# A six-layer attention pipeline on one core: the step's order rewritten on TensorE, ScalarE and VectorE

## The chip, the cores and the metric

The kernel runs on one core of a Trainium2 chip. The metric is the device time of one execution in microseconds (us). A core has five engines with a queue of instructions each: TensorE (PE; its weight loads are shown apart, as PEld), VectorE (DVE), ScalarE (ACT), GpSimd (POOL) and SyncE (SP), which here only starts DMAs. Each works its queue in order; they meet at semaphores. PE writes its results to PSUM, eight banks of 128 x 512 float32.

## The reference, cut to what matters

The program computes a chain of cross attentions and feed-forward networks on x (32 sequences of 128 tokens, 128 features). The change is in one part of it, six layers of local attention, each with a gated feed-forward network:

```
for i in range(6):
    x = attn_layer(shift_tokens(x), Wqkv[i], q_scale[i], k_scale[i], Wo[i]) + x
    x = ffn_layer(shift_tokens(x), ln_g[i], ln_b[i], W1[i], b1[i], W2[i], b2[i]) + x

def attn_layer(x, Wqkv, qs, ksc, Wo):        # 16 heads of 64
    q, k, v = jnp.split(x @ Wqkv, 3, -1)
    q = l2norm(q) * qs;  k = l2norm(k) * ksc
    q = q * cos * scale + rotate_half(q) * sin * scale
    k = k * cos / scale + rotate_half(k) * sin / scale
    return local_attention(q, k, v) @ Wo      # softmax, window of 32

def ffn_layer(x, g, bln, W1, b1, W2, b2):    # 128 -> 2 x 341 -> 128
    xn = (x - mu) / jnp.sqrt(var + 1e-05) * g + bln
    a, gate = jnp.split(xn @ W1 + b1, 2, -1)
    return a * gelu(gate) @ W2 + b2
```

shift_tokens moves the upper 64 features down by one token.

## The kernel before, in words

`layer_stack` holds the six layers. A tile is one sequence (128 tokens), so a layer has 32 tiles and the stack 192; four tiles are a quad, the unit of the feed-forward network. All engines run the same software pipeline (`layered_loop`): in step m each engine does pieces of work for several tiles, tile m (projection and rotation), m-1 (norms, turning of q and k), m-2 (values, scores, exponentials), m-3 and m-4 (turned probabilities, weighted values, output), m-5 and m-6 (token shift, layer norm). The order of the pieces in a step is written by hand for each engine in its `step` function; there is no scheduler. Every fourth step (k % 4 == 3) is a quad step, which also does the feed-forward network of an earlier quad. Of each layer the first 8 steps are unrolled (16 in the first), the others run in a hardware loop of 8 steps. After tile 191 there are 8 closing steps without new tiles.

The pieces that matter here, with their lines:

- PE. `project(m, j)` (L2646) makes the q or k unit j of tile m, 128 x 512 (units 0 and 1 are q, 2 and 3 are k). `project_values(m-2, half)` (L2663) makes half of the values. Both write to PSUM banks 0 and 1, which each result must leave before the next one. `shift(m-5)` (L2801) is a small matmul for the shifted tokens. `scores` (L2719, L2725), `turn_qk` (L2693), `turn_probs` (L2756), `weighted_values` (L2776), `output` (L2791), `turn_x` (L2614); in quad steps `turn_quad` (L2811), `hidden` (L2827, L2828), `ffn_output` (L2835).
- ACT. `squares` (L2334) reads a projected unit; `evacuate_values` half 1 (L2312), `evacuate_qk` (L2300), `evacuate_probs` (L2306), `evacuate_heads` half 0 (L2318), `exponentials` (L2326, four per group), `log_norms` and `over_norms` (L2340, L2345), `high_half` (L2363), which takes the result of `shift`, and `evacuate_x` (L2369, L2370), which writes the transposed input xsT of tile m.
- DVE. `maxima` (L2448), `evacuate_values` half 0 (L2496), `cosines` (L2462) and `sines` (L2473) of each unit, which wait for that unit's `squares`; `sums_of_squares` (L2480), `one_over_sums` (L2455), `statistics` (L2517), which waits for `high_half`, and `aggregate` (L2522).
- POOL. Its step, which the change leaves alone, runs one step of index ahead: `to_unit(n-3, 1)` (L2261), `keep(n-6)` (L2248), `to_unit(n-3, 3)`, `copy_for_values(n-3)` (L2235, xvT from xsT), `normalise(n-4, 0)` (L2268), `rotate(n-2, 2)` (L2254), `normalise(n-4, 1)`, `low_half` (L2241), `rotate(n-2, 3)`, `to_unit(n-2, 2)`, `to_unit(n-2, 0)`, `fetch(n)` (L2229), `rotate(n-1, 0)`, `rotate(n-1, 1)`, `normalise(n-4, 3)`, `normalise(n-4, 2)`.

xsT has two buffers, so `evacuate_x` of tile m+1 may write only when `copy_for_values` of tile m-1 has read the same buffer:

```
def evacuate_x(b, w, live):
    if live(b):
        act.wait_ge(turned, b + 1)
        wait(act, xvT_ready, b - 1)
```

`turn_qk` and `turn_probs` share banks 2 and 3, so `turn_qk(m-2, half 1)` waits until ACT has moved out what `turn_probs(m-4, half 1)` wrote just before it:

```
waits_alone(pe, env, (unit_ready[half], b + 1), (unit_ready[2 + half], b + 1),
            (probT_ready[1][0], b - 1), (probT_ready[1][1], b - 1))
```

## Time and profile before

| | |
|---|---|
| median of 3 runs | 4495.72 us (4494.81 to 4501.11) |
| the profiled execution | 4496.44 us, span 4494.6 us |
| busy over the span | PE 4166.5 us (93%), DVE 3761.2 (84%), ACT 3599.0 (80%), POOL 3142.6 (70%) |
| the six layers' projections (L2646) | from 563 us to 3764 us of the span |
| one regular step in the loop | 14.38 us, one quad step 23.00 us (2041.34 to 2055.72 and 2055.72 to 2078.72 us of the span) |

A busy share over the whole span mixes the six layers with the other parts. The six layers are one pipeline with a fixed period, so the trace is best read there one step at a time, from one `turn_x` on PE to the next.

### The profile page before, as it was taken

The page shows a single profiled execution, that of the slowest core. Times are in us where ns is not written, and L with a number is a line of the kernel's source. Part 1 is how long each engine was busy: PE and PEld are TensorE (multiplying, and loading weights), DVE is VectorE, ACT ScalarE, POOL GpSimd, SP SyncE. Part 2 cuts the span into 40 slices and gives each one's busy share as a digit, 9 for nine tenths or more (in the row PEclk, how much of TensorE's full clock was granted, in tenths as well). Part 3 has the DMA queues.
Part 4 walks back from the last instruction along what each step waited for, and adds up shares of the span by engine and source line. Part 5 has one row for each costly group of instructions (what it writes and reads, how often), then busy time and mean ns, then how long its engine had stood idle before and what let it go on. Part 6 is the DMA issues. An engine that isn't in the chain of part 4 may idle for free. (4 is left out here: it accounts for less than half of the span.)

```text
span 4494.6 us, 151390 instructions
## 1 busy us (share of the span) xinstructions
PE 4166.5 (93%) x51005; PEld 2759.3 (61%) x51005; DVE 3761.2 (84%) x9029; ACT 3599.0 (80%) x12939; POOL 3142.6 (70%) x4201
## 2 busy tenths in 40 slices
PE   6949999999999999999999999999999999677885
PEld 3426656666666666666666666666666666455543
DVE  4779989889889889889888889888889886688497
ACT  6938878888888888888888888888888887688335
POOL 2422288888879788889888788888888876444162
PEclk9969999999999999999999999999999999888886
DMA  2000000000000000000000000000000000000000
GB/s 63 0 21 1 0 8 2 2 3 16 13 3 2 3 21 8 3 3 9 14 8 3 3 12 12 8 3 3 16 12 3 3 3 2 1 0 0 29 1 19
DMA packets 38699, 37.87 MB, mean 8 GB/s; under 512 B 11382, under 2 KB 30068, under 8 KB 37748
## 3 DMA queue, kind: packets, MB, share of 16 engines
q1 hardware_dynamic: 38004, 28.97, 2.3%
q8 instruction: 391, 6.41, 0.6%
q14 instruction: 304, 2.49, 0.2%
HBM read 26.86 MB, written 2.10 MB: 6 GB/s over the span
## 5 line engine op out<-in xcount | busy, mean ns | idle before, releaser
L2326 ACT ACTIVATE stack_prob<-ps,stack_shift_by 128x128 f32<-128x128 f32 x3072 | 1078.7, 377 | 5.5 <-DVE stack_shift_by L2448 4.7
L2254 POOL TENSOR_TENSOR stack_qk<-stack_qk,stack_rsin 128x512 f32<-128x512 f32 x768 | 968.6, 1272 | 40.9 <-DVE stack_rsin L2473 40.9
L2261 POOL TENSOR_TENSOR stack_qk<-stack_qk,stack_inv 128x512 f32<-128x512 f32 x768 | 793.4, 1044 | 255.8 <-ACT stack_inv L2345 255.8
L2646 PE MATMUL ps<-local_wqkv,stack_xsT 128*128 128x512 f32 x1536 | 797.5, 601 | 7.1 <-DVE stack_vals L2496 3.0
L2268 POOL TENSOR_TENSOR stack_prob<-stack_prob,stack_rs 128x512 f32<-128x512 f32 x768 | 791.1, 1041 | 1.8 <-DVE stack_rs L2455 1.8
L2326 ACT ACTIVATION_READ_ACCUMULATOR stack_prob<-ps,stack_shift_by 128x1 f32 x3072 | 668.9, 218 | 0.0
L2448 DVE TENSOR_REDUCE stack_shift_by<-ps 128x4 f32<-128x512 f32 x768 | 524.3, 683 | 109.3 <-PE ps L2725 105.2
L2473 DVE TENSOR_TENSOR stack_rsin<-ps,stack_sin_t 128x256 f32<-128x256 f32 x1536 | 571.7, 413 | 0.0
L2462 DVE TENSOR_TENSOR stack_qk<-ps,stack_cos_t 128x512 f32<-128x512 f32 x768 | 525.2, 684 | 41.1 <-ACT stack_sq L2334 40.7
L2480 DVE TENSOR_REDUCE stack_ss<-stack_sq 128x8 f32<-128x512 f32 x768 | 514.0, 670 | 0.7 <-ACT stack_sq L2334 0.7
L2334 ACT ACTIVATE stack_sq<-ps 128x512 f32<-128x512 f32 x768 | 467.7, 609 | 50.8 <-PE ps L2646 43.9
L2306 ACT ACTIVATE stack_probT<-ps 128x512 f32<-128x512 f32 x768 | 427.4, 630 | 31.5 <-PE ps L2756 31.5
L2663 PE MATMUL ps<-local_wqkv,stack_xvT 128*128 128x512 f32 x768 | 433.4, 646 | 1.9 <-issue 1.6
L2776 PE MATMUL ps<-stack_probT,stack_vals 128*64 128x128 f32 x6144 | 425.6, 281 | 9.1 <-issue 7.0
L2776 PEld LDWEIGHTS ps<-stack_probT,stack_vals 128*64 128x64 f32 x6144 | 331.6, 138 | 165.7 <-issue 152.9
L2300 ACT ACTIVATE stack_qkT<-ps 128x512 f32<-128x512 f32 x384 | 230.9, 601 | 234.7 <-PE ps L2693 234.5
L2791 PE MATMUL ps<-local_wo,stack_oT 128*128 128x128 f32 x3072 | 389.0, 280 | 0.2 <-issue 0.2
L2791 PEld LDWEIGHTS ps<-local_wo,stack_oT 128*128 128x128 f32 x3072 | 361.2, 192 | 34.3 <-issue 24.5
L2646 PEld LDWEIGHTS ps<-local_wqkv,stack_xsT 128*128 128x128 f32 x1536 | 257.6, 191 | 179.0 <-issue 97.6
L2725 PE MATMUL ps<-stack_qkT 64*64 64x64 f32 (+1 forms) x12288 | 343.2, 232 | 0.0
L2725 PEld LDWEIGHTS ps<-stack_qkT 64*64 64x64 f32 x12288 | 311.1, 135 | 0.0
L2756 PEld LDWEIGHTS ps<-ident,stack_prob 64*128 64x128 f32 x6144 | 223.0, 139 | 94.8 <-issue 91.7
(342 smaller groups left out, 8601.7 us busy)
## 6 DMA issues: line engine op xcount, KB each, us to landing
local_wqkv<-L_ffn_Wqkv SPq DMA_DIRECT2D x30, 256.0 KB, 2.7
local_wo<-L_ffn_Wo SPq DMA_DIRECT2D x6, 512.0 KB, 4.5
out<-quantised_res SPq DMA_DIRECT2D x8, 256.0 KB, 2.3
local_w<-L_ffn_W SPq DMA_DIRECT2D x6, 341.0 KB
local_wqkv<-L_ffn_Wqkv SPq DMA_DIRECT2D x1, 1536.0 KB, 6.4
early_L_decay<-c_decay SPq DMA_DIRECT2D x1, 1024.0 KB, 10.7
local_w<-L_ffn_W SPq DMA_DIRECT2D x12, 64.0 KB
load_raw<-L_ffn_w SPq DMA_DIRECT2D x8, 64.0 KB, 2.0
```

What stands on the lines that cost most here:

```text
L2254: nc.gpsimd.tensor_tensor(qk[w][:, j, :, :], qk[w][:, j, :, :], rsin[j % 2][:, :, :], ALU.add).then_inc(rot_ready, 1)
L2261: nc.gpsimd.tensor_tensor(qk[w][:, j, :, :], qk[w][:, j, :, :], bcast(inv[:, w, 8 * j:8 * j + 8].unsqueeze(2), [P, 8, LH]), ALU.mult).then ...
L2268: nc.gpsimd.tensor_tensor(prob[w][:, g, :, :], prob[w][:, g, :, :], bcast(rs[:, w, HG * g:HG * g + HG].unsqueeze(2), [P, HG, P]), ALU.mult ...
L2326: last = nc.scalar.activation(prob[w][:, g, j, :], ps[:, 4 + g % 2, j * P:(j + 1) * P], ACT.Exp, bias=shift_by[:, w, h:h + 1], accum_out=s ...
L2448: nc.vector.tensor_reduce(shift_by[:, w, HG * g:HG * g + HG], bank, AX, ALU.max, negate=True).then_inc(shift_by_ready, 1)
L2462: nc.vector.tensor_tensor(qk[w][:, j, :, :], bank, bcast(cos_t[:, j // 2, :].unsqueeze(1), [P, 8, LH]), ALU.mult)
L2473: last = nc.vector.tensor_tensor(rsin[j % 2][:, :, o], bank[:, :, x], bcast(sin_t[:, j // 2, o].unsqueeze(1), [P, 8, 32]), ALU.mult)
L2480: nc.vector.tensor_reduce(ss[:, w, 8 * j:8 * j + 8, 0], sq[j % 2][:, :, :], AX, ALU.add).then_inc(ss_summed, 1)
L2646: nc.tensor.matmul(proj_bank(j), xsT[w][:, :], wqkv[:, 512 * j:512 * j + 512], start=True, stop=True).then_inc(proj_ready, 1)
L2725: last = nc.tensor.matmul(ps[part, 4 + p, j * P + keys.start:j * P + keys.stop], qkT[w][r, half, 0, j, part], qkT[w][r, half, 1, j, keys], ...
L2776: last = nc.tensor.matmul(PV[LH * p:LH * p + LH, j * P:(j + 1) * P], vals[w][:, LH * h:LH * h + LH], probT[w][:, 2 * half + p, j, :], star ...
L2791: last = nc.tensor.matmul(OUT[:, 0:P], oT[w][:, c, :], wo[:, c, :], start=c == 0, stop=c == 7)
```

## The change

The work of a step is the same, and no instruction on data is added or taken away; it is put in another order on PE, ACT and DVE. POOL and the DMAs keep theirs. On PE both value projections of tile m-2 and units 0 and 1 of tile m now stand together, behind the weighted values; unit 2 stands late, before the output. The units' banks change from (1, 0, 0, 1) to (0, 1, 0, 1), so that half 0 of the values and unit 0 use bank 0 one behind the other, and half 1 and unit 1 bank 1. The feed-forward network's hidden parts 0 and 2 use banks 0 and 6, part 1 banks 2 and 3. The waits follow the new order.

```diff
@@ -2161,14 +2161,14 @@
     PV, OUT = ps[:, 6, :], ps[:, 7, :]
 
 
-    UNIT_BANK = (1, 0, 0, 1)
+    UNIT_BANK = (0, 1, 0, 1)
     HALF_KEYS = (slice(0, LH), slice(32, P))
 
     def proj_bank(j):
         return ps[:, UNIT_BANK[j], :]
 
     def hidden_banks(c):
-        return (ps[:, 2, :], ps[:, 3, :]) if c != 1 else (ps[:, 1, :], ps[:, 6, :])
+        return (ps[:, 2, :], ps[:, 3, :]) if c == 1 else (ps[:, 0, :], ps[:, 6, :])
 
     def live_quad(q):
         return not isinstance(q, int) or 0 <= q < NQUADS
@@ -2387,36 +2387,38 @@
             def step(m, q, k, live, layer):
                 u, v = k % 2, 1 - k % 2
                 quad = k % QUAD == QUAD - 1 and live_quad(q - 2)
+                evacuate_x(m, u, live)
+                evacuate_probs(m - 4, u, 1, 0, live)
+                evacuate_probs(m - 4, u, 1, 1, live)
                 evacuate_heads(m - 4, u, 0, live)
-                evacuate_x(m, u, live)
+                exponentials(m - 2, u, 0, live)
+                exponentials(m - 2, u, 1, live)
+                evacuate_values(m - 2, u, 1, live)
+                log_norms(m - 1, v, live)
                 evacuate_qk(m - 2, u, 1, 0, live)
-                exponentials(m - 2, u, 0, live)
                 squares(m, u, 0, live)
-                log_norms(m - 1, v, live)
-                high_half(m - 5, v, live)
                 over_norms(m - 1, v, live)
                 squares(m, u, 1, live)
-                exponentials(m - 2, u, 1, live)
+                high_half(m - 5, v, live)
+                if quad:
+                    quad_input(q - 2, layer)
                 evacuate_probs(m - 3, v, 0, 1, live)
                 evacuate_probs(m - 3, v, 0, 0, live)
-                evacuate_values(m - 2, u, 1, live)
+                log_variance(m - 6, u, live)
                 if quad:
-                    quad_input(q - 2, layer)
-                log_variance(m - 6, u, live)
-                squares(m, u, 2, live)
-                over_deviation(m - 6, u, live)
-                if quad:
+                    over_deviation(m - 6, u, live)
                     gates(q - 2)
                     exponentials(m - 2, u, 2, live)
                     exponentials(m - 2, u, 3, live)
                     evacuate_qk(m - 1, v, 0, 0, live)
+                    squares(m, u, 2, live)
                 else:
+                    exponentials(m - 2, u, 2, live)
+                    over_deviation(m - 6, u, live)
+                    squares(m, u, 2, live)
+                    exponentials(m - 2, u, 3, live)
                     evacuate_qk(m - 1, v, 0, 0, live)
-                    exponentials(m - 2, u, 2, live)
-                    exponentials(m - 2, u, 3, live)
                 squares(m, u, 3, live)
-                evacuate_probs(m - 3, v, 1, 0, live)
-                evacuate_probs(m - 3, v, 1, 1, live)
             layered_loop(act, NB, step)
 
         @block.vector
@@ -2547,44 +2549,42 @@
                 if isinstance(m, int) and m % NB == 0 and live(m):
                     tables(m // NB)
                 maxima(m - 2, u, 0, live)
+                maxima(m - 2, u, 1, live)
+                bound_norms(m - 1, v, live)
                 evacuate_qk(m - 2, u, 1, 1, live)
+                evacuate_heads(m - 4, u, 1, live)
                 evacuate_values(m - 2, u, 0, live)
-                bound_norms(m - 1, v, live)
-                maxima(m - 2, u, 1, live)
                 one_over_sums(m - 3, v, 2, live)
                 one_over_sums(m - 3, v, 3, live)
+                one_over_sums(m - 2, u, 0, live)
+                statistics(m - 5, v, live)
+                one_over_sums(m - 2, u, 1, live)
+                aggregate(m - 5, v, live)
                 cosines(m, u, 0, live)
                 sines(m, u, 0, live)
+                maxima(m - 2, u, 2, live)
+                maxima(m - 2, u, 3, live)
                 cosines(m, u, 1, live)
                 sines(m, u, 1, live)
-                statistics(m - 5, v, live)
-                sums_of_squares(m, u, 0, live)
-                one_over_sums(m - 2, u, 0, live)
-                sums_of_squares(m, u, 1, live)
-                aggregate(m - 5, v, live)
-                evacuate_heads(m - 4, u, 1, live)
-                maxima(m - 2, u, 2, live)
-                one_over_sums(m - 2, u, 1, live)
                 if quad:
-                    maxima(m - 2, u, 3, live)
-                    sums_of_squares(m, u, 2, live)
                     gated(q - 2, 0, layer)
-                    cosines(m, u, 2, live)
+                    sums_of_squares(m, u, 0, live)
                     gated(q - 2, 1, layer)
-                    sines(m, u, 2, live)
+                    sums_of_squares(m, u, 1, live)
                     gated(q - 2, 2, layer)
                     residual(m - 4, u, layer, live)
                     norm(m - 6, u, (k - 6) % RING, live)
                     evacuate_qk(m - 1, v, 0, 1, live)
                     quad_residual(q - 2, layer)
                 else:
+                    sums_of_squares(m, u, 0, live)
                     evacuate_qk(m - 1, v, 0, 1, live)
-                    maxima(m - 2, u, 3, live)
-                    sums_of_squares(m, u, 2, live)
+                    sums_of_squares(m, u, 1, live)
                     residual(m - 4, u, layer, live)
                     norm(m - 6, u, (k - 6) % RING, live)
-                    cosines(m, u, 2, live)
-                    sines(m, u, 2, live)
+                cosines(m, u, 2, live)
+                sines(m, u, 2, live)
+                sums_of_squares(m, u, 2, live)
                 cosines(m, u, 3, live)
                 sines(m, u, 3, live)
                 sums_of_squares(m, u, 3, live)
@@ -2623,25 +2623,17 @@
                         keep_busy(nc, env, SPARE, FILL[(b, j)])
                     if j == 0:
                         pe.wait_ge(xsT_ready, b + 1)
-                        wait(pe, rot_step, 4 * b)
-                        if isinstance(b, int):
-                            wait(pe, vals_ready[1], b - 2)
-                            wait(pe, rot_step, 4 * b - 3)
-                    elif j == 1:
                         wait(pe, vals_ready[0], b - 1)
                         if isinstance(b, int):
                             wait(pe, rot_step, 4 * b - 1)
-                            wait(pe, rot_step, 4 * b - 2)
-                    elif j == 2:
-                        wait(pe, rot_step, 4 * b + 2)
-                        if isinstance(b, int):
-                            wait(pe, vals_ready[0], b - 1)
-                            wait(pe, rot_step, 4 * b - 1)
-                    else:
+                    elif j == 1:
                         wait(pe, vals_ready[1], b - 1)
                         if isinstance(b, int):
-                            wait(pe, rot_step, 4 * b + 1)
                             wait(pe, rot_step, 4 * b)
+                    elif j == 2:
+                        wait(pe, rot_step, 4 * b + 1)
+                    else:
+                        wait(pe, rot_step, 4 * b + 2)
                     new_layer(b, wq_loaded[j])
                     nc.tensor.matmul(proj_bank(j), xsT[w][:, :], wqkv[:, 512 * j:512 * j + 512],
                                      start=True, stop=True).then_inc(proj_ready, 1)
@@ -2649,16 +2641,9 @@
...
-                    if half == 0:
-                        wait(pe, rot_step, upto(4 * b + 7, 4 * TOTAL))
-                        if isinstance(b, int):
-                            wait(pe, rot_step, upto(4 * b + 6, 4 * TOTAL))
-                            wait(pe, vals_ready[0], b)
-                    else:
-                        wait(pe, rot_step, upto(4 * b + 9, 4 * TOTAL))
-                        if isinstance(b, int):
-                            wait(pe, rot_step, upto(4 * b + 8, 4 * TOTAL))
-                            wait(pe, vals_ready[1], b)
+                    wait(pe, rot_step, upto(4 * b + 7 + half, 4 * TOTAL))
+                    if isinstance(b, int):
+                        wait(pe, vals_ready[half], b)
...
@@ -2815,12 +2800,14 @@
...
+                        pe.wait_ge(rot_step, upto(4 * m + 1, 4 * TOTAL))
+                        if isinstance(q, int):
+                            pe.wait_ge(vals_ready[0], upto(m - 1, TOTAL))
+                        pe.wait_ge(oT_ready[1], upto(m - 3, TOTAL))
+                        pe.wait_ge(xT_ready, q + 1)
+                    elif c == 1:
-                        pe.wait_ge(xT_ready, q + 1)
-                    elif c == 1:
-                        pe.wait_ge(vals_ready[1], upto(m - 1, TOTAL))
-                        pe.wait_ge(oT_ready[1], upto(m - 3, TOTAL))
...
@@ -2847,25 +2834,26 @@
                 weighted_values(m - 4, u, 0, live)
                 scores(m - 2, u, 0, live)
                 turn_qk(m - 2, u, 1, live)
+                weighted_values(m - 4, u, 1, live)
                 project_values(m - 2, u, 0, live)
+                project_values(m - 2, u, 1, live)
                 project(m, u, 0, live)
                 shift(m - 5, v, live)
                 project(m, u, 1, live)
-                weighted_values(m - 4, u, 1, live)
-                turn_probs(m - 3, v, 0, live)
-                project_values(m - 2, u, 1, live)
                 if quad:
                     turn_quad(q - 2, m, k // QUAD)
-                project(m, u, 2, live)
+                turn_probs(m - 3, v, 0, live)
                 scores(m - 2, u, 1, live)
                 if quad:
                     hidden(q - 2, m, layer)
                     output(m - 4, u, live)
-                    wait_alone(pe, env, h_ready, 3 * (q - 2) + 3)
+                    wait_alone(pe, env, h_ready, 3 * (q - 2) + 2)
                     turn_qk(m - 1, v, 0, live)
                     ffn_output(q - 2)
+                    project(m, u, 2, live)
                 else:
                     turn_qk(m - 1, v, 0, live)
+                    project(m, u, 2, live)
                     output(m - 4, u, live)
                 project(m, u, 3, live)
             layered_loop(pe, NB, step)
```

PE, a regular step in the unrolled part of a layer, from `turn_qk` of tile m-2 (qk0) to the scores: xvT0 feeds the value projections, xsT0 the q and k projections. Before:

```order
L2693 MATMUL ps<-ident,stack_qk0 128x64 x16
L2663 MATMUL ps<-local_wqkv,stack_xvT0 128x512
L2646 MATMUL ps<-local_wqkv,stack_xsT0 128x512
L2801 MATMUL ps<-stack_xnew,shift 128x64
L2646 MATMUL ps<-local_wqkv,stack_xsT0 128x512
L2776 MATMUL ps<-stack_probT0,stack_vals0 64x128 x8
L2756 MATMUL ps<-ident,stack_prob1 128x64 x16
L2663 MATMUL ps<-local_wqkv,stack_xvT0 128x512
L2646 MATMUL ps<-local_wqkv,stack_xsT0 128x512
L2719 MATMUL ps<-band2,identb 64x4x64 x2
```

The same place now (line numbers are those of the changed kernel):

```order
L2678 MATMUL ps<-ident,stack_qk0 128x64 x16
L2761 MATMUL ps<-stack_probT0,stack_vals0 64x128 x8
L47 REGISTER_ALU
L2648 MATMUL ps<-local_wqkv,stack_xvT0 128x512
L47 REGISTER_ALU
L2648 MATMUL ps<-local_wqkv,stack_xvT0 128x512
L2638 MATMUL ps<-local_wqkv,stack_xsT0 128x512
L2786 MATMUL ps<-stack_xnew,shift 128x64
L2638 MATMUL ps<-local_wqkv,stack_xsT0 128x512
L2741 MATMUL ps<-ident,stack_prob1 128x64 x16
```

The weighted values moved ahead of the projections and the second value projection ahead of both units; unit 2 left this place.

DVE, a regular step from the copy of the values (vals) to `sines` of unit 1, with the semaphores that each waits for. Before:

```order
L2496 COPY stack_vals1<-ps 128x512 [waits stack_vproj_ready]
L2485 TENSOR_REDUCE stack_bounded<-stack_ss 128x32 [waits stack_ss_summed]
L2448 TENSOR_REDUCE stack_shift_by<-ps 128x4 [waits stack_scores_ready]
L2455 RECIPROCAL stack_rs<-stack_sm 128x4 [waits stack_exp_ready] x2
L2462 TENSOR_TENSOR stack_qk1<-ps,stack_cos_t 128x512 [waits stack_qk_turned,stack_sq_ready]
L2473 TENSOR_TENSOR stack_rsin0<-ps,stack_sin_t 128x8x32 [waits stack_rot_ready,stack_sq_ready]
L2473 TENSOR_TENSOR stack_rsin0<-ps,stack_sin_t 128x8x32
L2462 TENSOR_TENSOR stack_qk1<-ps,stack_cos_t 128x512 [waits stack_qk_turned,stack_sq_ready]
L2473 TENSOR_TENSOR stack_rsin1<-ps,stack_sin_t 128x8x32 [waits stack_rot_ready,stack_sq_ready]
```

Now:

```order
L2498 COPY stack_vals1<-ps 128x512 [waits stack_vproj_ready]
L2457 RECIPROCAL stack_rs<-stack_sm 128x4 [waits stack_exp_ready] x3
L2519 BN_STATS stack_stats<-stack_xs 128x6 [waits stack_shift_ready,stack_half_ready]
L2457 RECIPROCAL stack_rs<-stack_sm 128x4 [waits stack_exp_ready]
L2524 BN_AGGR stack_moments<-stack_stats 128x2 [waits stack_stats_ready]
L2464 TENSOR_TENSOR stack_qk1<-ps,stack_cos_t 128x512 [waits stack_qk_turned,stack_sq_ready]
L2475 TENSOR_TENSOR stack_rsin0<-ps,stack_sin_t 128x8x32 [waits stack_rot_ready,stack_sq_ready]
L2475 TENSOR_TENSOR stack_rsin0<-ps,stack_sin_t 128x8x32
L2450 TENSOR_REDUCE stack_shift_by<-ps 128x4 [waits stack_scores_ready] x2
L2464 TENSOR_TENSOR stack_qk1<-ps,stack_cos_t 128x512 [waits stack_qk_turned,stack_sq_ready]
L2475 TENSOR_TENSOR stack_rsin1<-ps,stack_sin_t 128x8x32 [waits stack_rot_ready,stack_sq_ready]
```

Both maxima of groups 0 and 1 now stand ahead of the copy, `statistics` (BN_STATS) stands ahead of the first cosines where it stood behind the sines of unit 1, and the maxima of groups 2 and 3 stand between units 0 and 1.

ACT, from the last `squares` of a step to the exponentials of group 0 in the next; probT0 are the turned probabilities, xsT0 the transposed input. Before:

```order
L2334 ACTIVATE stack_sq1<-ps 128x512 [waits stack_ss_summed,stack_proj_ready]
L2306 ACTIVATE stack_probT0<-ps 128x8x64 [waits stack_prob_turned] x2
L2318 ACTIVATE stack_oT0<-ps 128x512 [waits stack_pv_ready]
L2367 REGISTER_ALU
L2369 ACTIVATE stack_xsT0<-ps 64x128 [waits stack_xvT_ready,stack_turned]
L2370 ACTIVATE stack_xsT0<-ps 64x127
L2299 REGISTER_ALU
L2300 ACTIVATE stack_qkT0<-ps 128x8x64 [waits stack_qk_turned]
L2326 ACTIVATE stack_prob0,stack_sm<-ps,stack_shift_by 128x128 [waits stack_shift_by_ready]
```

Now:

```order
L2334 ACTIVATE stack_sq1<-ps 128x512 [waits stack_ss_summed,stack_proj_ready]
L2367 REGISTER_ALU
L2369 ACTIVATE stack_xsT0<-ps 64x128 [waits stack_xvT_ready,stack_turned]
L2370 ACTIVATE stack_xsT0<-ps 64x127
L2306 ACTIVATE stack_probT0<-ps 128x8x64 [waits stack_prob_turned] x2
L2318 ACTIVATE stack_oT0<-ps 128x512 [waits stack_pv_ready]
L2326 ACTIVATE stack_prob0,stack_sm<-ps,stack_shift_by 128x128 [waits stack_shift_by_ready]
```

`evacuate_x`, with its wait for xvT, now stands ahead of the evacuation of the turned probabilities.

## Rows read from the trace of the kernel before

**Rows 1.** Windows: stretch, its us, busy us (instructions) by engine, PE's granted clock, DMA.

```profile
2041.34:2055.72 14.38, 14.38 (x201) 9.85 (x200) 13.83 (x34) 12.97 (x53) 14.03 (x17) 1.00 0.01 3
2055.72:2078.72 23.00, 23.00 (x241) 15.05 (x240) 17.85 (x41) 18.94 (x62) 17.58 (x22) 1.00 0.01 2
```

**Rows 2.** Timeline of PE, regular step: start, us, engine, line, tiles, count.

```profile
2044.16 0.71 PE L2693 MATMUL ps<-ident,stack_qk 64*128 64x64 f32 x16
2044.80 1.13 PE L2663 MATMUL ps<-local_wqkv,stack_xvT 128*128 128x512 f32 x2
2045.77 1.02 PE L2646 MATMUL ps<-local_wqkv,stack_xsT 128*128 128x512 f32 x2
2046.62 0.33 PE L2801 MATMUL ps<-stack_xnew,shift 128*128 128x64 f32 x2
2046.79 1.08 PE L2646 MATMUL ps<-local_wqkv,stack_xsT 128*128 128x512 f32 x2
2047.80 1.09 PE L2776 MATMUL ps<-stack_probT,stack_vals 128*64 128x128 f32 x16
```

**Rows 3.** Timeline of DVE, the same step.

```profile
2045.97 0.69 DVE L2496 COPY stack_vals<-ps 128x512 f32<-128x512 f32 x1 [0.16 <-PE ps L2663]
2046.70 0.68 DVE L2448 TENSOR_REDUCE stack_shift_by<-ps 128x4 f32<-128x512 f32 x1
2047.30 0.23 DVE L2455 RECIPROCAL stack_rs<-stack_sm 128x4 f32<-128x4 f32 x2
2047.53 0.69 DVE L2462 TENSOR_TENSOR stack_qk<-ps,stack_cos_t 128x512 f32<-128x512 f32 x1
2048.14 0.75 DVE L2473 TENSOR_TENSOR stack_rsin<-ps,stack_sin_t 128x256 f32<-128x256 f32 x2
2050.06 0.28 DVE L2517 BATCH_NORM_STATS2 stack_stats<-stack_xs 128x6 f32<-128x128 f32 x1
```

**Rows 4.** Timeline of ACT, the same step.

```profile
2042.41 1.14 ACT L2306 ACTIVATE stack_probT<-ps 128x512 f32<-128x512 f32 x2
2043.84 0.30 ACT L2369 ACTIVATE stack_xsT<-ps 64x128 f32<-64x128 f32 x1
2044.15 0.27 ACT L2370 ACTIVATE stack_xsT<-ps 64x127 f32<-64x127 f32 x1
2047.52 0.21 ACT L2363 ACTIVATE stack_xs<-ps 128x64 f32<-128x64 f32 x1
2047.91 0.60 ACT L2334 ACTIVATE stack_sq<-ps 128x512 f32<-128x512 f32 x1
```

**Rows 5.** Timeline of POOL, the same step and the next's start.

```profile
2048.05 2.04 POOL L2261 TENSOR_TENSOR stack_qk<-stack_qk,stack_inv 128x512 f32<-128x512 f32 x2 [0.35 <-ACT stack_inv L2345]
2050.29 2.50 POOL L2254 TENSOR_TENSOR stack_qk<-stack_qk,stack_rsin 128x512 f32<-128x512 f32 x2
2057.15 0.29 POOL L2235 COPY stack_xvT<-stack_xsT 128x128 f32<-128x128 f32 x1
```

**Rows 6.** Timeline of PE, a quad step.

```profile
2064.80 0.60 PE L2811 MATMUL ps<-ident,XN 128*128 128x128 f32 x4
2067.14 1.13 PE L2827 MATMUL ps<-XN,local_w 128*128 128x512 f32 x2
2077.86 1.02 PE L2646 MATMUL ps<-local_wqkv,stack_xsT 128*128 128x512 f32 x2
```

**Rows 7.** Timeline of PE, the two steps behind the loop's jump.

```profile
2011.09 0.32 PE L2614 MATMUL ps<-ident,stack_xin 128*128 128x128 f32 x1 [0.98 <-issue]
2026.78 0.30 PE L2614 MATMUL ps<-ident,stack_xin 128*128 128x128 f32 x1
```

**Rows 8.** Windows where PE waited: in the layers' start, in a later part.

```profile
592.00:596.00 4.00, 1.82 (x21) 0.95 (x19) 3.80 (x8) 3.30 (x18) 3.83 (x6) 1.00 0.00 0
3940.00:3944.00 4.00, 2.12 (x16) 1.71 (x20) 4.00 (x8) 3.97 (x8) 1.61 (x2) 0.93 0.00 0
3944.00:3948.00 4.00, 4.00 (x96) 3.53 (x90) 2.80 (x6) 3.29 (x7) 2.75 (x10) 0.65 0.00 0
```

## The prediction

> **What bounds the kernel now.** I read the windows of single steps first, then the timeline of each engine inside one of them. In a regular step of 14.38 us PE is busy for all 14.38, DVE for 13.83, POOL for 14.03, ACT for 12.97; in the quad step of 23.00 us only PE is full [rows 1]. So the order before is bound by PE in both kinds of step, and the other engines' waits are short: 0.16 us of DVE ahead of the copy of the values [rows 3], 0.35 us of POOL ahead of `to_unit` [rows 5]. Two things follow. A better order of PE's work can only win what PE loses between its pieces, not idle time, since there is none. And DVE and POOL have 0.55 and 0.35 us to spare in a regular step, so an order that makes either wait longer than that makes the step longer, unless PE's work hides it, which it cannot: it is a loop of waits that sets the period then, not a busy engine.
>
> **What PE gains.** A pair of 512-column passes that comes behind small tiles takes 0.97 us from its start to the next (2044.80 to 2045.77), one behind another pair of the same shape 0.85 (2045.77 to 2046.62); the one ahead of the weighted values takes 1.01 (2046.79 to 2047.80) [rows 2]. The new order has about one such border less per step (both value projections and units 0 and 1 form one run; unit 2 runs into the output). I take 0.10 us a step, from the 0.12 between 0.97 and 0.85. The Trainium skill, TensorEngine Tiling (Array Packing), Key Properties, says that changing the tiling mode drains TensorE; these rows agree, and by that rule alone the change would be a small gain, the faster rival below.
>
> **What the order costs: a chain inside the step.** I call E the end of DVE's copy of value half 0.
> - Unit 0 now uses bank 0 right behind that half, so P0 (unit 0 of tile m) cannot start before E. Before, bank 1 was free for it and it started 0.97 us behind V0 with no wait.
> - PE: P0 0.96 (behind a wait I let it pay the border), shift 0.17, P1 to its end 1.08: 2.21 us [rows 2].
> - ACT: `squares` of unit 1 0.49 until `high_half` starts, which now stands behind it, and 0.21 for that: 0.70 [rows 4].
> - DVE: `statistics` now stands ahead of all cosines and waits for `high_half`.
> With three handoffs of 0.04 us each DVE gets to `statistics` 3.03 us after E. Between the two it has only three reciprocals, 0.3 us at 0.23 for two [rows 3]. So it waits 2.7 us in every regular step. DVE alone then needs 13.83 + 2.7 = 16.5 us a step.
>
> **The chain goes on and closes.** From `statistics` DVE does: it 0.28 less overlap, a reciprocal and `aggregate`, together 0.38; cosines 0 0.61; sines 0 0.66; maxima 2 and 3 at 0.60; cosines 1 0.61; sines 1 0.75: 4.2 us [rows 3]. Before, the sines of unit 1 came early, and the two maxima after them. POOL's `rotate(m, 1)` waits for these sines, and behind it in POOL's unchanged order stand two `normalise`, `to_unit`, `keep`, `to_unit` and `copy_for_values(m-1)`. From the second rotation's start (2050.29 plus half of 2.50) to the end of that copy (2057.15 + 0.29) is 5.90 us, without a wait in it [rows 5]. ACT's `evacuate_x(m+1)` needs that copy, since it writes the buffer which the copy reads. Before, it stood behind the evacuation of the probabilities and the heads; now it is first in the step, and everything of ACT's step is queued behind it. So follow on ACT 0.58 for `evacuate_x` and 1.12 for the two evacuations of probabilities: 1.70 [rows 4]. PE's `turn_qk(m-1, half 1)` needs banks 2 and 3 from those: 0.64, then the weighted values 1.02 (1.09 less the overlap of 0.07 that 0.71 against 0.64 shows), then V0 to its end 1.13: 2.79 [rows 2]. Then DVE copies V0 of the next step. The loop, for a shift of exactly one step:
> copy 0.69 + PE 2.21 + ACT 0.70 + DVE 4.2 + POOL 5.90 + ACT 1.70 + PE 2.79 = 18.2 us, and seven handoffs. A handoff is 0.04 us from PE to ACT (2046.79 + 1.08 to 2047.91) and 0.04 from PE to DVE (2044.80 + 1.13 to 2045.97) [rows 2 to 4]; the others are not in these rows. I take 0.05 each, the nearest value: 18.5 us. The bounds are 18.2 (none) and 19.2 (0.15 each, more than three times the two that are shown).
>
> The other engines fit into 18.5: PE works 14.3, DVE 13.8, POOL 14.0, ACT 13.0. The remaining new waits (unit 2 on the sines of unit 0, hidden part 0 on the same, `turn_qk` half 0 on the units that POOL makes from `over_norms`, which now comes 2 us after E) end before the chain needs them by my walk through the step; each has about 1 us or less to spare, and costs up to that if I am wrong. So a regular step goes from 14.38 to 18.5: +4.1 us.
>
> **A quad step.** The stretch of PE from the first hidden part to the projection behind the network's output is 10.72 us (2067.14 to 2077.86) [rows 6], and stays. Ahead of it now: copy 0.69, E to the end of `high_half` 3.0, for which `turn_quad` also waits, then on PE `turn_quad` 0.44 to 0.60 [rows 6], `turn_probs` and the scores about 1.6 (the first 0.64 as `turn_qk`). Behind it: unit 2 to its end 1.02, its square 0.60, and then on DVE, which is idle until then, cosines, sines and sum of units 2 and 3 (2 x 1.86, the sum taken as a maximum of 0.60), the maxima, the small reduction, two copies up to the next copy of V0 (2.5). The sum is 0.69 + 3.0 + 0.5 + 1.6 + 10.8 + 1.0 + 0.6 + 3.7 + 2.5 = 24.4 us, against 23.00. +1.5 us; bounds 0 and +3, since two of these terms are read from like pieces.
>
> **The sum.** Tiles 5 to 191 go through the whole loop: 187 steps, of which 46 are quad steps (11 to 191 by fours) and 141 regular. 141 x 4.1 = 580; 46 x 1.5 = 70. The hardware loop's jump happens 17 times (2 in the first layer, 3 in each other). Before, the step behind it takes 15.69 us (2011.09 to 2026.78) instead of 14.38, and PE stands 0.98 us at its start [rows 7]; in the new order part of that falls into waits and part on the chain. Between -25 and +20 us, I take 0. The first five and the closing steps: 0 to +10, I take 0. The profiled execution took 4496.44 us, 0.7 above the median of the runs. 4496 + 650 = 5146; I say 5140.
>
> **Rivals.**
> - TensorE's clock. PE will be busy 14.3 of 18.5 us instead of all the time, in stretches with two waits of about 1.7 us each. In this trace the clock was granted in full while PE was busy 1.82 of 4 us in the start of the layers, but it was 0.93 and then 0.65 in the mean (some of the time 1.2 GHz, the rest 2.4) around a stretch with 2.12 of 4 in a later part [rows 8], so both can happen at such a share. If it settled at 0.87 in the regular steps, the 5.0 us of PE in the loop would take 0.75 us longer: 141 x 0.75 = +105, so 5245. Against it: the waits stand between runs of long matmuls, as in the start of the layers. The Trainium skill, TensorE: Matmul & The Clock Gate, HAM oscillation, says that waits between short bursts bring the half clock back; it names no case with waits this short, and the trace is split.
> - Only the first chain holds: DVE waits 2.7 us, but `copy_for_values` comes in time, because POOL gains more than I see. Then the step is 16.5, 141 x 2.1 + 70 = 370, so 4866. What speaks against it is that sines 1, `normalise` and the copy are in fixed order and each wait is in the code.
> - PE stays the bound, and the change gives what it was worked out for above: 187 x 0.10 = 19 us, so 4477. It decides if DVE's new wait at `statistics` is under 0.55 us. Against it: P0 would have to start before E, which its wait forbids.
> - The new order is as slow as the old one within what can be told (0.2%, 9 us), the gain eaten by small waits: 4496. Same objection.
> - Half of DVE's wait and no more is left, because a piece of the chain runs beside another in a way that I don't see: 141 x 1.2 = 170, near 4665. Nothing in the rows points to such a piece.
>
> **How the numbers follow.** Chances: forecast 0.66, clock 0.13, DVE chain alone 0.09, partly hidden 0.06, no change 0.03, faster 0.03. The forecast's own range is 18.2 to 19.2 us a step, 5100 to 5240; with the quad step's bounds and small errors in each term 5010 to 5260. To leave out no more than two in ten, the range goes from 4930 (near the DVE chain alone) to 5270 (the clock). Slower 0.94, same 0.03, faster 0.03.
>
> **What would show it.** In the profile after: a regular step near 18.5 us and a quad step near 24.4; PE busy near 77% of a regular step; DVE idle about 2.7 us ahead of `statistics`, released by `high_half` on ACT; ACT idle for 2 to 4 us ahead of `evacuate_x`, released by POOL's copy; PE idle ahead of `turn_qk` half 1, released by the evacuated probabilities. If `evacuate_x` never waits for POOL, the second half of the chain is wrong and the time is near 4870. If DVE does not wait ahead of `statistics`, all of it is wrong. If pairs of passes that take 0.85 us now take twice that in places, it is the clock.

## The result

The changed kernel takes 5404.9 us (median of six runs, 5394.4 to 5412.8), the one before 4495.3 (six runs, 4492.0 to 4501.1): 1.202 times as long, 95% interval 1.2006 to 1.2037. It is 910 us slower. I had forecast 650 us slower, 5140, with a range up to 5270: the direction and the waits were right, the time lies outside the range.

### The profile page after: what moved, and what is told of

It is laid out like the page before. It is cut to its first block and busy times, and to the rows that moved or that the text cites. A ratio compares the mean times of both kernels' runs of the same rounds, so it can differ in the third digit from the quotient of the medians.

```text
span 5402.4 us, 151226 instructions
## 1 busy us (share of the span) xinstructions
PE 4485.7 (83%) x51003; PEld 2940.0 (54%) x51005; DVE 3812.3 (71%) x9029; ACT 3669.8 (68%) x12939; POOL 3158.5 (58%) x4201
## 5 line engine op out<-in xcount | busy, mean ns | idle before, releaser
L2638 PE MATMUL ps<-local_wqkv,stack_xsT 128*128 128x512 f32 x1536 | 823.7, 624 | 44.9 <-issue 17.1
L2450 DVE TENSOR_REDUCE stack_shift_by<-ps 128x4 f32<-128x512 f32 x768 | 493.2, 684 | 113.8 <-PE ps L2710 111.8
L2761 PE MATMUL ps<-stack_probT,stack_vals 128*64 128x128 f32 x6144 | 524.0, 324 | 5.8 <-issue 3.0
L2678 PE MATMUL ps<-ident,stack_qk 64*128 64x64 f32 x6144 | 289.3, 236 | 272.5 <-ACT stack_probT L2306 200.2
L2648 PE MATMUL ps<-local_wqkv,stack_xvT 128*128 128x512 f32 x768 | 464.6, 734 | 0.0
L2519 DVE BATCH_NORM_STATS2 stack_stats<-stack_xs 128x6 f32<-128x128 f32 x192 | 56.5, 294 | 569.9 <-ACT stack_xs L2363 569.9
L2678 PEld LDWEIGHTS ps<-ident,stack_qk 64*128 64x128 f32 x6144 | 241.8, 146 | 337.1 <-issue 299.1
L2761 PEld LDWEIGHTS ps<-stack_probT,stack_vals 128*64 128x64 f32 x6144 | 405.3, 160 | 35.3 <-issue 6.6
L2741 PE MATMUL ps<-ident,stack_prob 64*128 64x64 f32 x6144 | 276.8, 230 | 156.0 <-POOL stack_prob L2268 147.5
L2710 PE MATMUL ps<-stack_qkT 64*64 64x96 f32 (+1 forms) x12288 | 380.5, 246 | 0.7 <-issue 0.7
```

What stands on the lines that cost most here:

```text
L2450: nc.vector.tensor_reduce(shift_by[:, w, HG * g:HG * g + HG], bank, AX, ALU.max, negate=True).then_inc(shift_by_ready, 1)
L2638: nc.tensor.matmul(proj_bank(j), xsT[w][:, :], wqkv[:, 512 * j:512 * j + 512], start=True, stop=True).then_inc(proj_ready, 1)
L2678: last = nc.tensor.transpose(ps[:, 2 + p, (4 * i + c) * LH:(4 * i + c) * LH + LH], qk[w][r, 2 * i + half, 2 * c:2 * c + 2, :].rearrange("p ...
L2741: last = nc.tensor.transpose(ps[:, 2 + p, (4 * i + j) * LH:(4 * i + j) * LH + LH], prob[w][r, 2 * half + i, j, :], ident[r, r])
L2761: last = nc.tensor.matmul(PV[LH * p:LH * p + LH, j * P:(j + 1) * P], vals[w][:, LH * h:LH * h + LH], probT[w][:, 2 * half + p, j, :], star ...
```

## The profile after

| | before | after |
|---|---|---|
| profiled execution, its span | 4496.4, 4494.6 us | 5404.2, 5402.4 us |
| PE, DVE, ACT, POOL over the span | 93, 84, 80, 70% | 83, 71, 68, 58% |
| mean granted clock of TensorE | 0.958 | 0.912 |
| first to last q/k projection | 563.5 to 3764.2 us | 564.6 to 4664.7 us |

The last row holds nearly the whole loss: 3200.7 us for the 192 tiles before, 4100.1 after, +899. So one step of the loop is the place to read. These are rows of PE's timeline, in the same part of the first layer as [rows 2]: start, duration, what ran, and in brackets how long PE stood idle before it and who released it.

```profile
2017.47 1.98 PE L2648 MATMUL ps<-local_wqkv,stack_xvT 128*128 128x512 f32 x4
...
2034.74 0.71 PE L2678 MATMUL ps<-ident,stack_qk 64*128 64x64 f32 x16 [1.99 <-ACT stack_probT L2306]
2035.39 1.62 PE L2761 MATMUL ps<-stack_probT,stack_vals 128*64 128x128 f32 x16
2036.93 3.10 PE L2648 MATMUL ps<-local_wqkv,stack_xvT 128*128 128x512 f32 x4
2039.87 1.07 PE L2638 MATMUL ps<-local_wqkv,stack_xsT 128*128 128x512 f32 x2
...
2040.94 1.08 PE L2638 MATMUL ps<-local_wqkv,stack_xsT 128*128 128x512 f32 x2
...
2050.50 0.71 PE L2741 MATMUL ps<-ident,stack_prob 64*128 64x64 f32 x16 [1.03 <-POOL stack_prob L2268]
...
2055.16 0.34 PE L2678 MATMUL ps<-ident,stack_qk 64*128 64x64 f32 x4 [1.98 <-ACT stack_probT L2306]
...
2057.30 3.15 PE L2648 MATMUL ps<-local_wqkv,stack_xvT 128*128 128x512 f32 x4
...
2082.38 1.98 PE L2648 MATMUL ps<-local_wqkv,stack_xvT 128*128 128x512 f32 x4
```

From one step's value projections to the next step's it is 19.46, 20.37 and (a quad step) 25.08 us, where a step of [rows 1] took 14.38 and 23.00. PE, which had no wait in [rows 2], now stands 2 us ahead of `turn_qk` in two of these steps and 1 us ahead of `turn_probs`, beside shorter ones. And the same value projections (both halves, four passes) take 1.98 us in one step and 3.10 or 3.15 in others: those follow on a wait of 2 us, and the weighted values between (1.62) are stretched too, while the q and k projections 5 us behind the wait have their old 1.07. That is not work, it is the clock: in three windows of 2 us from 2036 on, the clock granted to PE (the figure behind the five engines' busy times) is 0.50, 0.70 and 1.00, with PE busy throughout.

```profile
2036.00:2038.00 2.00, 2.00 (x12) 1.16 (x9) 0.88 (x2) 1.72 (x10) 1.30 (x2) 0.50 0.00 0
2038.00:2040.00 2.00, 2.00 (x5) 0.82 (x4) 0.91 (x4) 0.00 (x0) 0.00 (x0) 0.70 0.00 0
2040.00:2042.00 2.00, 2.00 (x9) 0.76 (x7) 0.00 (x0) 1.90 (x5) 0.00 (x0) 1.00 0.04 8
```

It does not take a wait of 2 us. A little later the weighted values are slow (1.28 for 1.09) right behind a wait of 1.02, and then `turn_qk` behind one of only 0.79: PE's slow work has used up part of the wait.

```profile
2095.84 0.71 PE L2741 MATMUL ps<-ident,stack_prob 64*128 64x64 f32 x16 [1.02 <-POOL stack_prob L2268]
2096.47 1.28 PE L2761 MATMUL ps<-stack_probT,stack_vals 128*64 128x128 f32 x16
...
2100.29 1.12 PE L2678 MATMUL ps<-ident,stack_qk 64*128 64x64 f32 x16 [0.79 <-ACT stack_probT L2306]
```

The other three engines in the same step, DVE first:

```profile
2039.05 0.69 DVE L2498 COPY stack_vals<-ps 128x512 f32<-128x512 f32 x1 [1.31 <-PE ps L2648]
...
2042.87 0.29 DVE L2519 BATCH_NORM_STATS2 stack_stats<-stack_xs 128x6 f32<-128x128 f32 x1 [2.92 <-ACT stack_xs L2363]
...
2046.34 0.75 DVE L2475 TENSOR_TENSOR stack_rsin<-ps,stack_sin_t 128x256 f32<-128x256 f32 x2
```

ACT:

```profile
2042.06 0.60 ACT L2334 ACTIVATE stack_sq<-ps 128x512 f32<-128x512 f32 x1
2042.55 0.22 ACT L2363 ACTIVATE stack_xs<-ps 128x64 f32<-128x64 f32 x1
...
2053.19 0.27 ACT L2369 ACTIVATE stack_xsT<-ps 64x128 f32<-64x128 f32 x1 [2.44 <-POOL stack_xvT L2235]
...
2053.77 1.09 ACT L2306 ACTIVATE stack_probT<-ps 128x512 f32<-128x512 f32 x2
```

POOL:

```profile
2047.17 1.27 POOL L2254 TENSOR_TENSOR stack_qk<-stack_qk,stack_rsin 128x512 f32<-128x512 f32 x1 [1.19 <-DVE stack_rsin L2475]
...
2052.80 0.30 POOL L2235 COPY stack_xvT<-stack_xsT 128x128 f32<-128x128 f32 x1
```

Read in order of time these are one chain, each link beginning where the last ends: copy of value half 0 (end 2039.74), unit 0, shift and unit 1 on PE, squares and `high_half` on ACT (end 2042.77), `statistics` to the sines of unit 1 on DVE (4.22 us, end 2047.09), second rotation to `copy_for_values` on POOL (5.93 us, end 2053.10), `evacuate_x` and two evacuations on ACT (end 2054.86), `turn_qk`, weighted values and the next value projections on PE. No engine is full, and in this chain each waits for the one before it.

## The experiments

All are told by the median, and by the ratio to the kernel before run beside them on the same chip.

**Fill PE's gaps (fill).** Does the half clock cost time, or does it fall where PE would wait anyway?

```diff
+                    for _ in range(again):
+                        nc.tensor.matmul(proj_bank(j), xsT[w][:, :], wqkv[:, 512 * j:512 * j + 512], start=True, stop=True)
...
+                    keep_busy(nc, env, ps[:, 4, :], fill)
...
-                scores(m - 2, u, 0, live)
+                scores(m - 2, u, 0, live, 0 if k % QUAD == 0 else 5)
...
-                project(m, u, 3, live)
+                project(m, u, 3, live, 0 if k % QUAD == 3 else 1)
```

> The changed kernel with PE kept busy in two of its waits: in regular steps unit 3 is projected twice into its bank, and in each step but the one behind a quad step five 512-column bf16 matmuls are put ahead of the scores of half 0 (1.1 us), results as before. Theory A (the loop of waits, plus a TensorE clock that falls to 1.2 GHz in part of it): the granted clock in the layers goes from 0.93 to near 1.0, the regular step from about 20 to about 19 us, 5405 - 190 = 5215 us (5170 to 5270), and PE's waits are only filled. Theory B (the loop is longer than predicted by handoffs and waits alone, the clock costs nothing because its low stretches lie beside waits): the clock rises too, but the time stays at 5390 to 5420. Theory C (PE's own work binds): the added 2 us a step make it slower, 5600 or more.

Measured: 5245.1 us, ratio 1.166 (1.1641 to 1.1680), so 160 us less than the changed kernel although PE does more. PE's timeline, value projections of three steps:

```profile
2038.56 1.98 PE L2650 MATMUL ps<-local_wqkv,stack_xvT 128*128 128x512 f32 x4
...
2057.59 1.98 PE L2650 MATMUL ps<-local_wqkv,stack_xvT 128*128 128x512 f32 x4
...
2076.61 1.98 PE L2650 MATMUL ps<-local_wqkv,stack_xvT 128*128 128x512 f32 x4
```

All at full speed, 19.03 and 19.02 us apart. The windows 2000 to 3000 us of the changed kernel and then of this one (PE, PEld, DVE, ACT, POOL busy, granted clock, DMA):

```profile
2000.00:3000.00 1000.00, 848.78 (x9689) 562.46 (x9689) 691.36 (x1590) 683.99 (x2448) 655.96 (x743) 0.93 0.02 5
```

```profile
2000.00:3000.00 1000.00, 895.74 (x10346) 574.27 (x10347) 716.87 (x1649) 710.75 (x2527) 679.26 (x771) 0.99 0.02 6
```

The clock goes from 0.93 to 0.99, and DVE, ACT and POOL get some 4% more done. The half clock costs about 160 us. The loop of waits alone, at full clock, makes the step 19.03 us and the kernel 5245. The changed kernel's own trace agrees. Here are two of its steps in a row, from one step's value projections to the next's:

```profile
1740.20:1759.24 19.04, 14.90 (x202) 9.94 (x200) 14.21 (x33) 13.40 (x53) 13.04 (x16) 1.00 0.00 1
1759.24:1778.28 19.04, 16.44 (x202) 11.23 (x200) 13.96 (x33) 13.21 (x51) 14.10 (x17) 0.91 0.01 3
```

The first has the full clock and takes 19.04 us. The second has 0.91 and takes no longer: there the slow work lies ahead of the wait for `turn_qk`, which is 0.23 us instead of 1.77. The half clock costs time only where it meets PE's pieces of the loop, behind that wait.

**Undo one order at a time.** Three edits to the changed kernel, each of which should shorten the loop at one place: `evacuate_x` behind ACT's evacuations and heads (evacx_back), `statistics` and `aggregate` behind the sines of unit 1 (stats_back), the two maxima behind them (maxima_back).

```diff
                 quad = k % QUAD == QUAD - 1 and live_quad(q - 2)
-                evacuate_x(m, u, live)
                 evacuate_probs(m - 4, u, 1, 0, live)
                 evacuate_probs(m - 4, u, 1, 1, live)
                 evacuate_heads(m - 4, u, 0, live)
+                evacuate_x(m, u, live)
```

```diff
-                statistics(m - 5, v, live)
                 one_over_sums(m - 2, u, 1, live)
-                aggregate(m - 5, v, live)
...
                 sines(m, u, 1, live)
+                statistics(m - 5, v, live)
+                aggregate(m - 5, v, live)
```

```diff
-                maxima(m - 2, u, 2, live)
-                maxima(m - 2, u, 3, live)
                 cosines(m, u, 1, live)
                 sines(m, u, 1, live)
+                maxima(m - 2, u, 2, live)
+                maxima(m - 2, u, 3, live)
```

> The changed kernel with one thing undone on ACT: evacuate_x stands behind the evacuated probabilities and heads again. Theory A (the whole loop over POOL's copy_for_values sets the period): turn_qk half 1 comes 2.0 us earlier in a regular step, so 141 x 2.0 = 280 us less, and some of the clock's loss with it: 5000 to 5130 us. Theory B (DVE's wait ahead of statistics alone sets it): no change, 5390 to 5420.

> The changed kernel with statistics and aggregate behind the sines of unit 1 again on DVE. Theory A (the loop): cosines of unit 0 start behind the square of unit 0 instead of behind high_half, 1.5 us earlier, and every later piece of the loop with them: 141 x 1.5 = 210 less, 5195 us (5130 to 5250). DVE's wait moves to the cosines, 1.2 to 1.8 us, released by squares. Theory B (something on PE or the clock sets the period): 5380 to 5420.

> The changed kernel with the maxima of groups 2 and 3 behind the sines of unit 1 on DVE. DVE's busy time and its wait ahead of statistics stay as they are. Theory A (the loop goes over the sines to POOL): 1.2 us less per regular step, 141 x 1.2 = 170 less, 5235 us (5180 to 5280). Theory B (DVE's busy time plus its wait sets the period): no change, 5390 to 5420.

| | us | ratio (95%) | against the changed kernel |
|---|---|---|---|
| evacx_back | 4992.8 | 1.110 (1.1078 to 1.1115) | -412 |
| stats_back | 5099.8 | 1.134 (1.1318 to 1.1356) | -305 |
| maxima_back | 5123.7 | 1.139 (1.1370 to 1.1408) | -281 |

Each gave more than expected; the clock came back as well (0.98, 0.99 and 0.97 in the same window). The three sum to -998, more than the whole loss of 910, and together, below, they give -603. One reason is the clock: each of the three takes most of its 160 us back, and together they can do that only once. To see the loop without it, I read the commonest regular step whose clock is granted in full: 17.19, 17.92 and 17.82 us, against 19.02 in fill. That is 1.83, 1.10 and 1.20 less, near what I had expected of each piece (2.0, 1.5 and 1.2). With all three undone it is 16.06: 2.96 less where the three sum to 4.13, so by then something else sets the step. The summary of waits (engine, line, releaser: us in all, times, longest), 2000 to 3000 us, of evacx_back:

```profile
DVE stack_stats L2519 <- ACT stack_xs L2363: 156.6, 52, 4.6
...
ACT stack_xsT L2369 <- POOL stack_xvT L2235: 8.8, 32, 0.3
```

and of stats_back:

```profile
DVE stack_qk L2464 <- ACT stack_sq L2334: 89.7, 62, 1.7
...
ACT stack_xsT L2369 <- POOL stack_xvT L2235: 74.6, 38, 2.0
```

The first leaves DVE's wait (3.0 us a step) as it was and still wins the most: DVE's wait alone does not make the step. The second takes that wait away and finds DVE waiting for `squares` instead.

**Pairs and all three.** evacx_maxima_back and evacx_stats_back hold two of the edits, three_back all.

> Two undone at once in the changed kernel: evacuate_x behind the heads, maxima 2 and 3 behind the sines of unit 1. Alone these gained 412 and 281 us. Theory A (the period is that of the longest loop; with the copy off the path the loop is DVE's own work, 13.8 us, plus its wait of 2.9 ahead of statistics, on which the maxima's place has no effect): 4960 to 5000 us, hardly below the 4993 of the first edit alone. Theory B (gains add up): 5405 - 412 - 281 = 4712.

> Two undone at once in the changed kernel: evacuate_x behind the heads, statistics and aggregate behind the sines. Theory A: DVE's wait by the bank (about 1.75 us ahead of the cosines) plus its work is the longest loop, as in the kernel with all three undone: 4790 to 4840 us against its 4802. Theory B (each edit keeps its own gain of 305): 4688.

> The changed kernel with all three undone at once: evacuate_x behind probabilities and heads, statistics and aggregate behind the sines of unit 1, maxima 2 and 3 behind these. PE's order and the banks stay as changed. Theory A: the loop over POOL is gone as a bound; what is left is DVE's chain by the bank: copy of value half 0, unit 0, its square, cosines, 1.75 us of waiting on DVE beside 13.8 busy, so 15.6 to 15.9 us a regular step: 4496 + 141 x 1.35 + 46 x 1.2 = 4740 us (4670 to 4800). Theory B (the single gains only add up): 5405 - 412 - 305 - 281 = 4407, faster than before. Theory C (the grouped PE order itself costs, by its borders and banks): above 4850.

| | us | ratio (95%) |
|---|---|---|
| evacx_maxima_back | 5045.4 | 1.121 (1.1193 to 1.1231) |
| evacx_stats_back | 4914.8 | 1.093 (1.0914 to 1.0951) |
| three_back | 4801.8 | 1.067 (1.0655 to 1.0690) |

Once `evacuate_x` is back, the maxima's edit makes it 53 us worse and not better. PE's timeline shows what makes the step longer, first of evacx_back, then with the maxima's edit added:

```profile
2115.47 0.71 PE L2741 MATMUL ps<-ident,stack_prob 64*128 64x64 f32 x16 [1.02 <-POOL stack_prob L2268]
```

```profile
2116.14 0.71 PE L2741 MATMUL ps<-ident,stack_prob 64*128 64x64 f32 x16 [1.24 <-ACT stack_qkT L2300]
```

ACT now waits longer for the maxima (149.7 us in the window, where evacx_back has 92.0), its exponentials of groups 2 and 3 are late, and `evacuate_qk`, which stands behind them in ACT's order, releases PE 0.2 us later than POOL did. A regular step at full clock goes from 17.19 to 17.40, which is some 30 of the 53 us. Most of the rest lies in steps behind a quad step: 30 of the 46 now have a low clock, where it was 20, and such a step takes 19.5 us for 17.6. I had left this out, and both pairs missed their expectation. three_back too, at 4802, is just above the 4670 to 4800 of its theory A. With all three the granted clock is 1.00 in the window and 306 us stay, with these waits:

```profile
DVE stack_qk L2464 <- ACT stack_sq L2334: 90.2, 68, 1.6
...
PE ps L2741 <- ACT stack_qkT L2300: 40.5, 41, 1.1
```

So the rest is in what these edits leave as the change made it: PE's order and the remaining order of ACT and DVE. The runs don't part it further.

**The same edits done alone to the kernel before.** before_evacx_front puts `evacuate_x` first and both late evacuations behind it; before_stats_front puts `high_half` behind the squares of unit 1 and `statistics` ahead of the cosines.

```diff
+                evacuate_x(m, u, live)
+                evacuate_probs(m - 4, u, 1, 0, live)
+                evacuate_probs(m - 4, u, 1, 1, live)
                 evacuate_heads(m - 4, u, 0, live)
-                evacuate_x(m, u, live)
...
                 squares(m, u, 3, live)
-                evacuate_probs(m - 3, v, 1, 0, live)
-                evacuate_probs(m - 3, v, 1, 1, live)
```

```diff
-                high_half(m - 5, v, live)
                 over_norms(m - 1, v, live)
                 squares(m, u, 1, live)
+                high_half(m - 5, v, live)
...
+                statistics(m - 5, v, live)
                 cosines(m, u, 0, live)
```

> The kernel before with one part of the change alone: on ACT evacuate_x stands first in the step, ahead of the evacuated probabilities and heads. Theory A (a wait ahead of queued work costs what exceeds the slack): evacuate_x cannot start before POOL's copy ends, so the probabilities leave 0.8 us later, turn_qk half 1 starts 0.8 us later and PE, which has no slack, loses about 0.7 us in each regular step: 4496 + 100 = 4595 us (4550 to 4640). Theory B (harmless where the order of DVE is the old one, since POOL catches up): 4490 to 4510.

> The kernel before with another part alone: on DVE statistics ahead of the cosines of unit 0, on ACT high_half behind the square of unit 1; the banks and PE's order are those of before. Theory A: DVE waits about 1.1 us ahead of statistics in each regular step, of which 0.55 is slack; 141 x 0.6 = 80 us more, 4576 us (4530 to 4630), a quarter or less of what the same two edits cost in the changed kernel, where unit 0 waits for DVE's copy. Theory B (this wait is what makes the changed kernel slow whatever the banks): DVE waits 2.5 us or more and the time is above 4750.

Measured: 4615.4 us, ratio 1.026 (1.0238 to 1.0272), as expected, and 4720.9 us, ratio 1.049 (1.0475 to 1.0510), between both theories. The two sum to +340, of the 910. In the second DVE waits 1.2 us a step, about what I said (1.1), but PE waits 0.8 us in a regular step at a place that I had not followed; waits of before_stats_front, 2000 to 3000 us:

```profile
DVE stack_stats L2517 <- ACT stack_xs L2363: 67.7, 55, 2.4
...
PE ps L2663 <- DVE stack_rsin L2473: 33.6, 39, 1.5
```

In the banks of before, value half 1 needs bank 1 from the sines of unit 0, and these now stand behind `statistics`.

**Can PE's grouping be kept?** grouped_retuned keeps PE's new order and banks and moves ACT and DVE so that each piece stands where its input comes: what both chains wait for goes first. grouped_retuned_2 is a second such version: beside smaller moves, ACT makes POOL's scale factors earlier and the layer norm goes to the next step. Each is shown in part.

```diff
-                evacuate_x(m, u, live)
                 evacuate_probs(m - 4, u, 1, 0, live)
                 evacuate_probs(m - 4, u, 1, 1, live)
                 evacuate_heads(m - 4, u, 0, live)
+                evacuate_x(m, u, live)
+                evacuate_qk(m - 2, u, 1, 0, live)
...
+                high_half(m - 5, v, live)
                 over_norms(m - 1, v, live)
                 squares(m, u, 1, live)
-                high_half(m - 5, v, live)
...
                 sines(m, u, 1, live)
+                statistics(m - 5, v, live)
                 one_over_sums(m - 2, u, 0, live)
                 sums_of_squares(m, u, 0, live)
+                aggregate(m - 5, v, live)
```

```diff
+                norm(m - 7, v, (k - 7) % RING, live)
                 one_over_sums(m - 3, v, 2, live)
...
                     residual(m - 4, u, layer, live)
-                    norm(m - 6, u, (k - 6) % RING, live)
```

> A version of my own on the grouped PE order and the new banks: ACT takes evacuate_x behind the heads, high_half early, and unit 2's square ahead of exponentials 2; DVE puts the sum of unit 3, the small reduction and the copy of the heads between its copy of value half 0 and the cosines, and statistics and maxima 2 and 3 behind the sines of unit 1. Theory A: work lies in DVE's wait by the bank, so a regular step is 14.4 to 14.9 us and the time 4490 to 4600. Theory C (the banks' chain costs whatever stands in it): 15.5 us or more, above 4700.

> A second version on the grouped PE order: the small reduction, log_norms and over_norms come before the values' evacuation, so that POOL gets its scale factors 1.5 to 2 us earlier than in grouped_retuned (whose PE waits 0.74 us for POOL's units ahead of turn_qk half 0); DVE puts the layer norm of tile m-7 and the heads' copy in its wait; ACT does exponentials 1 behind the square of unit 0. Theory A (POOL's late scale factors made the 15.5 us step): 14.5 to 14.9 us, 4510 to 4580. Theory C (another wait takes its place, exponentials 1 ahead of the scores of half 1): 15.2 to 15.6, 4610 to 4660.

Measured: 4648.2 us, ratio 1.033 (1.0311 to 1.0346), between its two theories, and 4728.3 us, ratio 1.051 (1.0495 to 1.0530), worse than both of its. The first wins back 757 of the 910 us with PE's new order and banks untouched, so these are not in themselves what costs most. No run takes the order and the banks apart. What is left in it is on PE,

```profile
PE ps L2677 <- POOL stack_qk L2261: 28.4, 41, 0.7
```

0.7 us a step for units that POOL makes late. In the second POOL waits for the moved layer norm, 2.3 us a step in the mean, where the first has no such wait. That this wait makes the step longer is likely but not shown, since other pieces moved with it:

```profile
POOL stack_xs L2241 <- DVE XN L2529: 131.3, 56, 6.4
```

No version here beats the kernel before.

## Why the prediction was half right

- **"What PE gains", 0.10 us a step.** Of no consequence: PE waits in every step of the changed kernel, so what it saves between its pieces is waited away.
- **"A chain inside the step".** Right. DVE was to reach `statistics` 3.03 us after the copy's end and wait 2.7; it got there 3.13 after (2042.87 less 2039.74) and waited 2.92. (The 0.49 us of `squares` in that sum stands in none of its rows; it is what the changed kernel shows, 2042.06 to 2042.55.)
- **"The chain goes on and closes".** Right in every link, and evacx_back, stats_back and maxima_back each shorten it, at full clock by 1.83, 1.10 and 1.20 us. The pieces were sized well: DVE 4.22 for 4.2, POOL 5.93 for 5.90, ACT 1.67 for 1.70. The term that was off is the seven handoffs, taken as 0.05 us each from the two in [rows 2 to 4]. In the step above they are 0.13, 0.04, 0.10, 0.08, 0.09, 0.30 and 0.05, in all 0.79 for 0.35. In a step of fill (2039.73 to 2058.75) they are some 0.67, with 0.14 for the 0.30, and DVE's piece is 4.40 for 4.2. So of the 0.5 by which a regular step at full clock is over the forecast, 19.03 for 18.5, about 0.3 is handoffs and 0.2 DVE. 141 x 0.53 = 75 us. The forecast's own bound of 19.2 a step held.
- **"A quad step", 24.4.** Four steps take 81.8 us in the fill run, so the quad step 81.8 - 3 x 19.03 = 24.7: 0.3 more, 46 x 0.3 = 14. The stretch from the first hidden part to the projection behind the output, 10.72 us, is 10.71 now (2065.47 to 2076.18).
- **"The sum", loop jumps 0.** Eight steps with one jump take 167.2 us in the fill run (from one `copy_for_values` to the eighth behind it, 2135.48 to 2302.68), 3.6 more than two times 81.8; before, they take 134.9, 2.6 more than two times 66.14. So a jump costs 1.0 us more, 17 us in all. The forecast's 5146 and these three, 75, 14 and 17, are 5252; fill has 5245.
- **"Rivals: TensorE's clock".** This is the step that failed. I gave it as an alternative to the forecast, with a chance of 0.13, on the ground that the waits stand between runs of long matmuls and that the first stretch of [rows 8] kept the full clock at 45% busy. It came on top of the forecast: 0.93 granted, with stretches at 1.2 GHz behind waits of 1 to 2 us, and 160 us (the difference of the changed kernel and fill) where I had priced 105 for it. I was right that it is the 5 us of PE in the loop that pay: value projections 3.10 for 1.98 and weighted values 1.62 for 1.09 are 1.7 us in a step where it happens, and 160/187 = 0.86 in the mean of all steps, for the 0.75 that I took. But I took it from a mean clock of 0.87, and the measured one is higher, 0.92 in the step from 2028.75 to 2049.17; the low stretches do not fall evenly but often just on these pieces, behind the wait. The range ended near what this rival gave (5245), and what the handoffs add was not put on top of it. The Trainium skill, TensorE: Matmul & The Clock Gate, HAM oscillation, says that waits between bursts of work bring the half clock back; its case has longer waits than the 1 to 2 us here, and the trace shows it with these too.
- **"DVE chain alone", "half hidden", "no change", "faster".** All fell: ACT waits for POOL's copy 2.44 us, as the second half of the chain has it.

Of the 910 us, 650 are the forecast's steps, 106 the terms mis-sized, and 160 the clock. That these come to 916 leaves nothing for another cause of size, but the handoffs and the jump were read from single steps and one loop and not changed alone, and the three terms were taken from the fill run after the fact. Why 306 us stay in three_back is only named by its waits, not tested.

## What to carry to other kernels

When several engines are nearly full in a pipeline written by hand, the period is the larger of the fullest engine and the longest loop of waits divided by the steps it spans: walk each new wait forward until it closes or dies out, and give each handoff about 0.1 us and not the best one seen. Edits to pieces of one loop add up only until another loop is the longest (4.1 us a step by the single runs, 3.0 together), and with one gone another edit can turn from gain to loss; so test edits in pairs. And if the walk ends with TensorE waiting 1 to 2 us at a time just ahead of its pieces of the loop, its clock is a term of the sum and not a rival to it.

## What the runs showed of the hardware

- Four 512-column passes took 1.98 us at full clock and 3.10 to 3.15 behind a wait of 2 us on TensorE (granted clock 0.50 and 0.70 in the two windows there); 5 us behind the wait a pair took its old 1.07 again. Elsewhere it fell behind a wait of 1.02. The granted clock was 0.93 over 1000 us with TensorE busy for 849, and 0.99 with 896.
- A step with a granted clock of 0.91 took 19.04 us, as one with 1.00 did, since the slow work took the place of a wait.
- TensorE started 0.30 us after ACT's end behind a wait of 1.98 us, but 0.14 behind one of 1.77 (2185.18 to 2185.32) and behind one of 0.58 (in fill); the other handoffs of the loop took 0.03 to 0.15.
- Useless matmuls in the gaps made the kernel 160 us faster (5405 to 5245), since waits set the period and TensorE had time for them.
